# One mixture-of-experts kernel: the transposes of the next expert's rows, in blocks of eight or one by one between the gate/up matmuls

## The chip, the cores and the metric

The kernel runs on one core of one Trainium2 chip, in one launch. The metric is the time of the core in microseconds (us). The kernel before takes 2088.13 us, the median of 3 runs (2086.33 to 2092.45).

## The reference, cut to what matters

There are two stages. First an attention layer without values: the softmaxed scores of `ctx_512` (4 batches of 1024 rows) are multiplied by a tanh gate and added to `x` (4096 rows of 1024). Then each row goes through a mixture of experts:

```
logits = x @ gate_w.T                      # 64 experts
w, sel = top_k(softmax(logits), 8)
xin[e, slot] = x[tok]                      # up to 256 rows per expert
h   = silu(xin @ wg[e]) * (xin @ wu[e])    # 1024 -> 384
out = h @ wd[e]                            # 384 -> 1024
y[tok] += w * out
```

All inputs are float32. The result is `x + tanh(g) * y`. The change touches only the second stage.

## The kernel before, in words

**Attention and routing** (the first fifth of the time) compute the rows, the choice of experts and a table that says which row goes to which slot of which expert. The normalised rows are stored in DRAM as `h_rows`.

**The expert stage** goes through 64 experts one after the other. It keeps float32 accuracy with bf16 matmuls: every float32 operand is split into a high bf16 part and a low bf16 remainder, and three of the four products are summed (`PAIRS`, line 442). ScalarE (ACT) makes the high parts and VectorE (DVE) the low ones. For one expert `e`, in buffer set `u = e % 2`:

- GpSimd (POOL) gathers the 256 rows into `xg[u]` with two indirect DMAs (line 956), and at the end adds the expert's output rows into `out` (line 980).
- TensorE (PE) transposes those rows: 16 transposes of 128x128, in four quarters `q` of four (`turn`, line 431). Quarter `q` goes to the PSUM tile `ps_x[q % 2]`, so that two quarters fill both tiles and the third needs the first tile back. This happens while the expert before is being computed.
- ACT copies a turned quarter to bf16 (`turned_high`, line 621, instruction 623) and DVE makes its low part (`turned_low`, line 850, instruction 852). The latter increments `xT_out`, four times an expert; it is what frees the PSUM tile for PE.
- PE computes gate and up for three column groups `m` = 0, 1, 2 (`gate_up`, line 444): 48 matmuls of 256 columns each (8 `k` steps, 3 pairs, for gate and for up), and increments `gu_done` on the last one. Group `m` of expert `e` has its own PSUM tile `ps_gu[m]`.
- ACT computes silu of the group (`silu`, line 617, instruction 619) and DVE multiplies it with up, and splits the product (`activate`, line 841, instructions 846 to 848).
- PE computes the down projection (`down`, line 469, instruction 463): 36 matmuls of 512 columns. ACT scales the results (`rows_out`, line 625).

**The order on PE** of one expert (lines 487 to 493) is: group m = 0 (48 matmuls), transposes of quarters 0 and 1 of expert `e + 1` (8), group m = 1 (48), transposes of quarters 2 and 3 (8), group m = 2 (48), down (36). Before the transposes of a quarter PE waits twice (lines 433 and 435): until the rows are gathered, and until `xT_out` has reached `4 * e + q - 1`, where `e` is the expert whose rows are turned. For q = 2 this says that DVE is done with quarter 0 of the same expert, for q = 0 that it is done with quarter 2 of the expert before.

Each engine works through its own list in order; nothing overtakes. The lists of ACT and DVE aren't touched by the change. For one expert they are

```
# ACT, lines 638 to 654                    # DVE, lines 856 to 871
down_high(e, 0); down_high(e, 1)           down_low(e, 0); down_low(e, 1)
silu(e, 0)                                 activate(e, 0)
turned_high(e+1, q=0), (q=1)               turned_low(e+1, q=0), (q=1)
gate_high(e+1, 0), (1)                     gate_low(e+1, 0), (1)
silu(e, 1)                                 activate(e, 1)
turned_high(e+1, q=2), (q=3)               turned_low(e+1, q=2), (q=3)
up_high(e+1, 0)                            up_low(e+1, 0)
silu(e, 2)                                 activate(e, 2)
up_high(e+1, 1); rows_out(e)               up_low(e+1, 1)
```

Here `silu(e, m)` waits for `gu_done` of group m, `activate(e, m)` for that silu, `turned_high` for the transposes of its quarter, and `turned_low` for `turned_high`. The sync queue (SP) loads the weights of later experts (lines 340 to 348), behind the low parts that free their buffers.

Of the kernel before, what the change touches and what calls it, by code (L numbers as in the profile page):

```python
# [30 lines left out]
P = 128  # L31
# [44 lines left out]
def flamingo_moe(nc, x, ctxT, mask, kpm, g_x, g_f, wqT, bqT, wkT, bkT, gwT, wg, wu, wd, out):  # L76
    B, CP, CC, S = ctxT.shape
    T, H = x.shape
    E, _, KH, I = wg.shape
    MI = I // P  # L80
    TB = S // P
# [12 lines left out]
    with ExitStack() as ctx:  # L94
        def sem(name):
            return ctx.enter_context(nc.semaphore(name))

        def sb(name, shape, dt, where=ctx):
            return where.enter_context(nc.sbuf_tensor(name, shape, dt))
# [5 lines left out]
        ident = sb("ident", [P, P], F32)  # L105
# [58 lines left out]
        xg = [sb(f"xg{u}", [P, 2, HW], F32) for u in range(2)]  # L164
# [55 lines left out]
        gathered = [sem(f"gathered{u}") for u in range(2)]  # L220
        wcol_ready = sem("wcol_ready")
        xT_done = sem("xT_done")
        xT_high = sem("xT_high")
        xT_out = sem("xT_out")
# [21 lines left out]
        ps_x = [ps(f"ps_x{i}", [P, 2, CAP], F32, ctx) for i in range(2)]  # L246
# [7 lines left out]
        def attention_done(eng):  # L254

            eng.wait_ge(routed, N)
            for i in range(4):
                eng.wait_ge(x1_stored[i], 16 * N // 4)
                eng.wait_ge(h_stored[i], 16 * N // 4)
# [99 lines left out]
        def _(pe):  # L359
# [68 lines left out]
                    project(g // TB + 1, g % TB)  # L428


            def turn(e, u, q, first=False):

                pe.wait_ge(gathered[u], 16 * (e - u) + 32)
                if not (first and q < 2):
                    pe.wait_ge(xT_out, 4 * e + q - 1)
                for kk in range(2):
                    for half in range(2):
                        at = (2 * q + kk) * P
                        mm = pe.transpose(ps_x[q % 2][:, kk, half * P:(half + 1) * P], xg[u][:, half, at:at + P], ident[:])  # L439
                mm.then_inc(xT_done, 1)  # L440

            PAIRS = ((0, 0), (0, 1), (1, 0))

            def gate_up(e, u, m, first=False):
                if not first:
                    pe.wait_ge(act_ready, MI * e - MI + m + 1)
                for t, w in ((0, split_g[u]), (1, split_u[u])):
                    if m == 0:
                        pe.wait_ge((g_low, u_low)[t], 2 * e + 2)
                    for k in range(KH):  # L450
                        if m == 0 and t == 0 and k % 2 == 0:
                            pe.wait_ge(xT_out, 4 * e + k // 2 + 1)
                        for wi, xi in PAIRS:
                            mm = pe.matmul(ps_gu[m][:, t, :], w[:, wi, k, m * P:(m + 1) * P], xT[u][:, k, xi, :],  # L454
                                           start=(k == 0 and (wi, xi) == (0, 0)),
                                           stop=(k == KH - 1 and (wi, xi) == (1, 0)))
                mm.then_inc(gu_done, 1)

            def down_part(u, n, ms):
                half, c = n // 2, n % 2  # L460
                for m in ms:
                    for wi, ai in PAIRS:
                        mm = pe.matmul(ps_d[n % 3][:], act[u][:, ai, m, half * P:(half + 1) * P],  # L463
                                       split_d[:, wi, m, c * NH:(c + 1) * NH],
                                       start=(m == 0 and (wi, ai) == (0, 0)),
                                       stop=(m == MI - 1 and (wi, ai) == (1, 0)))
                return mm

            def down(e, u, first=False):

                pe.wait_ge(d_low, 2 * e + 2)
                pe.wait_ge(act_ready, MI * e + MI - 1)
                for n in range(2):
                    if not first:

                        pe.wait_ge(down_out, 4 * e - 2 * n)
                    down_part(u, n, range(MI - 1))
                pe.wait_ge(act_ready, MI * e + MI)
                for n in range(2):
                    down_part(u, n, [MI - 1]).then_inc(down_done, 1)  # L480
                if not first:
                    pe.wait_ge(down_out, 4 * e - 1)
                down_part(u, 2, range(MI)).then_inc(down_done, 1)
                pe.wait_ge(down_out, 4 * e + 1)
                down_part(u, 3, range(MI)).then_inc(down_done, 1)

            def expert(e, u, first=False, last=False):
                for m in range(MI):
                    gate_up(e, u, m, first)
                    if m < 2 and not last:  # L490
                        turn(e + 1, 1 - u, 2 * m)
                        turn(e + 1, 1 - u, 2 * m + 1)
                down(e, u, first)

            attention_done(pe)
            for q in range(4):
                turn(0, 0, q, True)
            expert(0, 0, True)
            with pe.Fori(0, E // 2 - 1) as i:
                expert(2 * i + 1, 1)  # L500
                expert(2 * i + 2, 0)
# [543 lines left out]
```

## Time and profile before

| | |
|---|---|
| median of 3 runs | 2088.13 us (2086.33 to 2092.45) |
| profiled execution | the page gives its span alone, 2089.3 us |
| PE busy | 1924.5 us, 92% |
| DVE busy | 1313.1 us, 63% |
| ACT busy | 1143.8 us, 55% |
| POOL busy | 811.9 us, 39% |
| PE transposes (line 439) | 1024, 273 ns each as recorded |
| PE gate/up matmuls (line 454) | 9216 of 256 columns, 273 ns each as recorded |
| PE down matmuls (line 463) | 2304 of 512 columns, 379 ns each as recorded |

The recorded duration of a matmul is its way through the array. Matmuls overlap, so what one costs is the distance between the starts of two neighbours. "PEld" is the loading of the stationary operand, which overlaps the matmul before. The time in brackets at the end of a timeline row is how long the engine stood idle before it, and on what.

### The profile page before, as it was taken

The numbers are of one execution on the slowest core, as the hardware profiler recorded it, in microseconds if no ns is written. First come the engines' busy times: TensorE is split into PE (matmuls) and PEld (weight loads), VectorE is DVE, ScalarE is ACT, GpSimd is POOL, SyncE is SP. The second block draws the span as 40 slices with busy tenths as digits, with TensorE's granted clock in tenths as the row PEclk, the third lists the DMA queues.
The fourth block names the chain that finished last, engine by engine and source line by source line (L and its number), as shares of the span: only waits on it lengthen the run. The fifth ranks groups of instructions, "written<-read, shape, count | busy, mean of one in ns | idle before, by whom it ended". The sixth has DMA issues, their size and how long they took to land.

```text
span 2089.3 us, 37900 instructions
## 1 busy us (share of the span) xinstructions
PE 1924.5 (92%) x13696; PEld 1429.0 (68%) x13760; DVE 1313.1 (63%) x2221; ACT 1143.8 (55%) x1507; POOL 811.9 (39%) x751
## 2 busy tenths in 40 slices
PE   7777777529999999999999999999999999999998
PEld 3444444427777777777777777777777777777775
DVE  5766666536666666666666666666666666666663
ACT  5555555425555555555555555555555555555553
POOL 0788788762323332333232333322222322332321
PEclk9999997659999999999999999999999999999999
DMA  5465443227888888888888888888888888888883
GB/s 219 150 237 185 134 137 134 94 77 248 272 275 276 279 277 279 276 278 276 264 264 267 270 266 270 275 276 278 278 278 278 278 278 266 264 266 269 267 269 74
DMA packets 90632, 501.27 MB, mean 240 GB/s; under 512 B 17761, under 2 KB 19553, under 8 KB 65505
## 3 DMA queue, kind: packets, MB, share of 16 engines
q1 hardware_dynamic: 45536, 362.24, 43.7%
q0 software_dynamic: 45056, 138.58, 29.9%
q8 instruction: 16, 0.26, 0.1%
q14 instruction: 24, 0.19, 0.0%
HBM read 396.69 MB, written 104.07 MB: 240 GB/s over the span
## 4 chain that ended last, share of the span: by engine, by line
PE 78%; POOL 11%; issue 8%; DMA 1%; POOLq 0%; DVE 0%; ACT 0%; SPq 0%; DVEq 0%
PE ps_gu L454 48%; PE ps_d L463 24%; POOL place_table L923 10%; PE ps_x L439 5%; POOL norm L916 1%; PE ps_j L369 0%; PE ps_s L380 0%; DMA b_qk<-in_bqT 0%; PE ps_t L369 0%; DMA xg<-h_rows,g_idx 0%; POOLq L923 0%; DMA place_table<-token_no,where 0%; POOLq L94 0%; DMA table<-place_table 0%; DVE xb L792 0%
## 5 line engine op out<-in xcount | busy, mean ns | idle before, releaser
L980 POOL DMA_INDIRECT out<-ob,s_idx x128 | 207.2, 1619 | 1051.5 <-ACT ob L632 1029.8
L454 PE MATMUL ps_gu<-xT,split_g 128*128 128x256 bf16 x4608 | 536.2, 273 | 0.0
L454 PE MATMUL ps_gu<-xT,split_u 128*128 128x256 bf16 x4608 | 534.4, 273 | 0.0
L463 PE MATMUL ps_d<-split_d,act 128*128 128x512 bf16 x2240 | 493.9, 379 | 3.4
L454 PEld LDWEIGHTS ps_gu<-xT,split_g 128*128 128x128 bf16 x4608 | 451.9, 98 | 65.1
L454 PEld LDWEIGHTS ps_gu<-xT,split_u 128*128 128x128 bf16 x4608 | 450.9, 98 | 52.2
L838 DVE TENSOR_TENSOR split_d<-raw_d,split_d 128x1536 bf16<-128x1536 f32 x128 | 219.3, 1755 | 398.6 <-ACT split_d L615 398.6
L463 PEld LDWEIGHTS ps_d<-split_d,act 128*128 128x128 bf16 x2304 | 225.4, 98 | 258.2
L923 POOL DMA_INDIRECT place_table<-token_no,where x256 | 294.0, 1148 | 77.6 <-issue 77.3
L619 ACT ACTIVATE sil<-ps_gu 128x256 f32<-128x256 f32 x192 | 73.7, 384 | 445.3 <-PE ps_gu L454 445.3
L632 ACT ACTIVATE ob<-ps_d,wcol 128x512 f32<-128x512 f32 x256 | 171.3, 687 | 259.0 <-PE ps_d L463 259.0
L833 DVE TENSOR_TENSOR split_u<-raw_u,split_u 128x1536 bf16<-128x1536 f32 x128 | 225.0, 1758 | 16.8 <-ACT split_u L608 10.3
L828 DVE TENSOR_TENSOR split_g<-raw_g,split_g 128x1536 bf16<-128x1536 f32 x128 | 219.5, 1756 | 4.7 <-ACT split_g L601 4.5
L956 POOL DMA_INDIRECT xg<-h_rows,g_idx x128 | 184.1, 1438 | 74.9 <-POOL g_idx L953 51.9
L608 ACT ACTIVATE split_u<-raw_u 128x1536 bf16<-128x1536 f32 x128 | 189.3, 1480 | 0.0
L601 ACT ACTIVATE split_g<-raw_g 128x1536 bf16<-128x1536 f32 x128 | 182.8, 1484 | 4.2 <-DMA h_rows<-hrow 4.2
L615 ACT ACTIVATE split_d<-raw_d 128x1536 bf16<-128x1536 f32 x128 | 182.1, 1473 | 0.0
L852 DVE TENSOR_TENSOR xT<-ps_x,xT 128x512 bf16<-128x512 f32 x256 | 164.2, 682 | 24.2 <-ACT xT L623 24.2
L846 DVE TENSOR_TENSOR prod<-sil,ps_gu 128x256 f32<-128x256 f32 x192 | 80.8, 421 | 151.4 <-ACT sil L619 150.5
L439 PE MATMUL ps_x<-ident,xg 128*128 128x128 f32 x1024 | 134.5, 275 | 34.6 <-DMA xg<-h_rows,g_idx 34.0
L623 ACT ACTIVATE xT<-ps_x 128x512 bf16<-128x512 f32 x256 | 139.3, 595 | 33.2 <-PE ps_x L439 26.6
L439 PEld LDWEIGHTS ps_x<-ident,xg 128*128 128x128 f32 x1024 | 117.1, 142 | 36.7 <-issue 35.1
(86 smaller groups left out, 1426.0 us busy)
## 6 DMA issues: line engine op xcount, KB each, us to landing
raw_g<-in_wg SPq DMA_DIRECT2D x64, 1536.0 KB, 11.6
raw_u<-in_wu SPq DMA_DIRECT2D x64, 1536.0 KB, 15.7
raw_d<-in_wd SPq DMA_DIRECT2D x64, 1536.0 KB
h_rows<-hrow SPq DMA_DIRECT2D x34, 544.0 KB, 3.6
xb<-in_x SPq DMA_DIRECT2D x32, 512.0 KB, 5.0
out<-xb SPq DMA_DIRECT2D x32, 512.0 KB, 2.7
ctx_sb<-in_ctxT SPq DMA_DIRECT2D x4, 1024.0 KB, 8.7
place_table<-token_no,where POOLq DMA_INDIRECT x256
```

Source lines behind the costliest of these rows:

```text
L439: mm = pe.transpose(ps_x[q % 2][:, kk, half * P:(half + 1) * P], xg[u][:, half, at:at + P], ident[:])
L454: mm = pe.matmul(ps_gu[m][:, t, :], w[:, wi, k, m * P:(m + 1) * P], xT[u][:, k, xi, :], start=(k == 0 and (wi, xi) == (0, 0)), stop=(k == ...
L463: mm = pe.matmul(ps_d[n % 3][:], act[u][:, ai, m, half * P:(half + 1) * P], split_d[:, wi, m, c * NH:(c + 1) * NH], start=(m == 0 and (wi, ...
L601: s.activation(split_g[u][:, 0, ks], raw_g[u][:, ks], ACT.Copy).then_inc(g_high, 1)
L608: s.activation(split_u[u][:, 0, ks], raw_u[u][:, ks], ACT.Copy).then_inc(u_high, 1)
L615: s.activation(split_d[:, 0, :, cs], raw_d[:, :, cs], ACT.Copy).then_inc(d_high, 1)
L828: v.tensor_tensor(split_g[u][:, 1, ks], raw_g[u][:, ks], split_g[u][:, 0, ks], ALU.subtract).then_inc(g_low, 1)
L833: v.tensor_tensor(split_u[u][:, 1, ks], raw_u[u][:, ks], split_u[u][:, 0, ks], ALU.subtract).then_inc(u_low, 1)
L838: v.tensor_tensor(split_d[:, 1, :, cs], raw_d[:, :, cs], split_d[:, 0, :, cs], ALU.subtract).then_inc(d_low, 1)
L923: p.indirect_dma_start(out=place_table, out_offset=bass.IndirectOffsetOnAxis(ap=where8[u][:, k:k + 1].bitcast(U32), axis=0), in_=token_no[ ...
L956: p.indirect_dma_start(out=xg[u][:, half, :], out_offset=None, in_=h_rows, in_offset=bass.IndirectOffsetOnAxis(ap=g_idx[u][:, half:half + ...
L980: p.indirect_dma_start(out=out, out_offset=bass.IndirectOffsetOnAxis(ap=s_idx[u][:, half:half + 1].bitcast(U32), axis=0), in_=ob[u][:, hal ...
```

## The change

The diff replaces `turn`, which issued the four transposes of a quarter together, by `turn_one`, which issues one transpose `at` (0 to 15; quarter `at // 4`). The two waits stand ahead of the first transpose of a quarter and the increment of `xT_done` on its last, as before. `gate_up` now takes a list of transposes and issues one of them after every fifth of its 48 matmuls until the list is used up. Transposes 0 to 7 (quarters 0 and 1) go into group m = 0, behind its matmuls 5, 10, ... 40, and transposes 8 to 15 (quarters 2 and 3) into group m = 1, likewise. The 16 transposes of expert 0, ahead of the first matmul, stay together.

```diff
-            def turn(e, u, q, first=False):
-
-                pe.wait_ge(gathered[u], 16 * (e - u) + 32)
-                if not (first and q < 2):
-                    pe.wait_ge(xT_out, 4 * e + q - 1)
-                for kk in range(2):
-                    for half in range(2):
-                        at = (2 * q + kk) * P
-                        mm = pe.transpose(ps_x[q % 2][:, kk, half * P:(half + 1) * P], xg[u][:, half, at:at + P], ident[:])
-                mm.then_inc(xT_done, 1)
+            def turn_one(e, u, at):
+
+                q, k, half = at // 4, at // 2, at % 2
+                if at % 4 == 0:
+                    pe.wait_ge(gathered[u], 16 * (e - u) + 32)
+                    if not (isinstance(e, int) and e == 0 and q < 2):
+                        pe.wait_ge(xT_out, 4 * e + q - 1)
+                mm = pe.transpose(ps_x[q % 2][:, k % 2, half * P:(half + 1) * P],
+                                  xg[u][:, half, k * P:(k + 1) * P], ident[:])
+                if at % 4 == 3:
+                    mm.then_inc(xT_done, 1)
...
-            def gate_up(e, u, m, first=False):
+            def gate_up(e, u, m, first=False, turns=()):
                 if not first:
                     pe.wait_ge(act_ready, MI * e - MI + m + 1)
+                turns, n = list(turns), 0
...
+                            n += 1
+                            if not turns or n % TURN_EVERY:
+                                continue
+                            turn_one(e + 1, 1 - u, turns.pop(0))
+                assert not turns
                 mm.then_inc(gu_done, 1)
...
+            TURN_EVERY = 5
+            TURNS = (range(0, 8), range(8, 16), ())
+
             def expert(e, u, first=False, last=False):
                 for m in range(MI):
-                    gate_up(e, u, m, first)
-                    if m < 2 and not last:
-                        turn(e + 1, 1 - u, 2 * m)
-                        turn(e + 1, 1 - u, 2 * m + 1)
+                    gate_up(e, u, m, first, () if last else TURNS[m])
                 down(e, u, first)
 
             attention_done(pe)
-            for q in range(4):
-                turn(0, 0, q, True)
+            for at in range(16):
+                turn_one(0, 0, at)
```

## Rows read from the trace of the kernel before

**Rows 1.** The page, part 4: the chain that ended last, by engine.
```profile
PE 78%; POOL 11%; issue 8%; DMA 1%; POOLq 0%; DVE 0%; ACT 0%; SPq 0%; DVEq 0%
```

**Rows 2.** Windows: length, busy time of PE, PEld, DVE, ACT, POOL; then PE clock.
```profile
100.00:200.00 100.00, 73.67 (x307) 44.24 (x306) 66.91 (x250) 57.36 (x104) 81.47 (x72) 0.91 0.63 218
...
490.00:1500.00 1010.00, 1007.90 (x7804) 774.62 (x7843) 648.20 (x760) 569.69 (x681) 311.62 (x281) 1.00 0.84 273
1500.00:2040.00 540.00, 538.90 (x4185) 415.18 (x4204) 346.70 (x407) 305.90 (x365) 161.40 (x151) 1.00 0.84 271
```

**Rows 3.** Timeline of PE over one expert: start, length, what, count.
```profile
1223.32 2.78 PE L454 MATMUL ps_gu<-xT,split_g 128*128 128x256 bf16 x24
1225.94 2.78 PE L454 MATMUL ps_gu<-xT,split_u 128*128 128x256 bf16 x24
1228.56 1.04 PE L439 MATMUL ps_x<-ident,xg 128*128 128x128 f32 x8
1229.43 2.78 PE L454 MATMUL ps_gu<-xT,split_g 128*128 128x256 bf16 x24
...
1234.67 1.04 PE L439 MATMUL ps_x<-ident,xg 128*128 128x128 f32 x8
...
1241.00 7.72 PE L463 MATMUL ps_d<-split_d,act 128*128 128x512 bf16 x35
1248.55 0.71 PE L454 MATMUL ps_gu<-xT,split_g 128*128 128x256 bf16 x5
```

**Rows 4.** Timeline of ACT over the same expert.
```profile
1228.76 0.38 ACT L619 ACTIVATE sil<-ps_gu 128x256 f32<-128x256 f32 x1 [1.81 <-PE ps_gu L454]
1229.19 1.09 ACT L623 ACTIVATE xT<-ps_x 128x512 bf16<-128x512 f32 x2
...
1234.87 0.38 ACT L619 ACTIVATE sil<-ps_gu 128x256 f32<-128x256 f32 x1 [1.85 <-PE ps_gu L454]
```

**Rows 5.** Timeline of DVE over the same expert.
```profile
1229.27 0.42 DVE L846 TENSOR_TENSOR prod<-sil,ps_gu 128x256 f32<-128x256 f32 x1 [0.24 <-ACT sil L619]
1229.73 0.37 DVE L847 CAST act<-prod 128x256 bf16<-128x256 f32 x1
1230.13 0.42 DVE L848 TENSOR_TENSOR act<-prod,act 128x256 bf16<-128x256 f32 x1
1230.47 1.28 DVE L852 TENSOR_TENSOR xT<-ps_x,xT 128x512 bf16<-128x512 f32 x2
1231.68 3.43 DVE L828 TENSOR_TENSOR split_g<-raw_g,split_g 128x1536 bf16<-128x1536 f32 x2
...
1236.41 1.28 DVE L852 TENSOR_TENSOR xT<-ps_x,xT 128x512 bf16<-128x512 f32 x2
```

**Rows 6.** Timelines of DVE, PE and PEld: the one wait of PE for `xT_out`.
```profile
461.86 0.69 DVE L852 TENSOR_TENSOR xT<-ps_x,xT 128x512 bf16<-128x512 f32 x1 [22.79 <-ACT xT L623]
...
462.69 1.94 PE L439 MATMUL ps_x<-ident,xg 128*128 128x128 f32 x8 [0.65 <-DVE xT L852]
...
462.66 1.57 PEld L439 LDWEIGHTS ps_x<-ident,xg 128*128 128x128 f32 x8 [1.02 <-issue]
```

**Rows 7.** The gather of an expert's rows: POOL's timeline, and the landing times.
```profile
1228.25 1.75 POOL L956 DMA_INDIRECT xg<-h_rows,g_idx  x1 [0.84 <-POOL g_idx L953]
1230.31 1.15 POOL L956 DMA_INDIRECT xg<-h_rows,g_idx  x1 [0.31 <-issue]
...
DMA to landing us min/median/max: 10.0/12.9/15.0
```

**Rows 8.** Timeline of PE in the attention stage, behind two of its gaps.
```profile
217.33 1.09 PE L390 MATMUL ps_t<-ident,hrow 128*128 128x128 f32 x8 [2.74 <-ACT hrow L549]
218.26 1.88 PE L369 MATMUL ps_j<-ctx_sb,w_qk 128*128 128x512 f32 x4
...
292.64 1.10 PE L390 MATMUL ps_t<-ident,hrow 128*128 128x128 f32 x8 [2.42 <-ACT hrow L549]
293.58 3.19 PE L369 MATMUL ps_j<-ctx_sb,w_qk 128*128 128x512 f32 x4
```

## The prediction

> **What bounds the kernel now.** I began with the chain of waits [rows 1]: PE carries 78% of what ended last, and most of the rest (POOL, issue) belongs to the routing stage, which the change leaves alone. Then I asked for busy time by stretch [rows 2]. In the expert stage PE is busy 1007.90 of 1010.00 us and 538.90 of 540.00, at full clock (1.00); no other engine there passes 65%, since DVE has 648.20 of 1010. Last I laid out one expert [rows 3]. The starts follow each other without a gap. From 1225.94 to 1228.56 there are 24 matmuls in 2.62 us, 0.1092 us each; from 1228.56 to 1229.43 eight transposes in 0.87 us, 0.109 each. Expert to expert, 1223.32 to 1248.55, is 25.23 us. The 144 gate/up matmuls and 16 transposes at 0.1092 make 17.47; what is left, 7.76 us for 36 down matmuls, is 0.216 each. The rows show 35 of these because one record is missing; counting 36, nothing is left for idling. So in this stage PE never waits, it does the same number of instructions after the change, and every wait that is new to PE is paid in full, 63 times (once for each expert that has a successor). Nothing that becomes faster on ACT or DVE can pay it back.
>
> **Part 1: single transposes instead of blocks.** A single transpose is followed by a bf16 matmul and preceded by one. Both neighbourhoods exist already, at the two ends of each block of eight. Were either change of type dear, the block would take longer than eight steps; it takes 0.87 us, eight steps at 0.1092 being 0.874, and the second block is the same. I take zero. Per expert there are 4 changes of type now and 32 afterwards. Rounding of the rows hides at most 0.01 us in two changes, so 28 more are worth -0.14 to +0.14 us an expert, -9 to +9 us over 63.
>
> The rows give 0.109 us for a transpose of 128 float32 columns, as much as for a matmul of 256 bf16 columns [rows 3]; no row shows a transpose that stands alone, and I carry the same price over. The Trainium skill, page "TensorE: Matmul & The Clock Gate", section "Back-to-back issue gap", puts a warm matmul at its columns over 2.4 GHz and 2.5 ns, 56 ns for 128 columns; by that rule transposes would cost half, and the sum would be 55 us lower if it came to hold once they stand alone. The trace does not agree for float32 transposes in blocks; the sum goes by the trace.
>
> **Part 2: the end of group m = 0 moves back.** Its eight transposes now lie before its last matmul instead of behind it, so `gu_done` comes 8 x 0.109 = 0.87 us later. The same holds for m = 1. Waiting for it is ACT's silu, and ACT was idle for 1.81 and 1.85 us just before [rows 4]; DVE waited 0.24 us for silu [rows 5]. These engines start 0.87 us later and have no one behind them that PE needs before the next groups: the low parts of the gate weights, 1231.68 to 1235.11, end at 1235.98 and are wanted by the next expert at 1248.6. The shift itself costs nothing. What it feeds is part 3.
>
> **Part 3: the wait for quarter 2 moves forward.** This is the step that decides. Transpose 8 needs the PSUM tile of quarter 0, that is `xT_out` from DVE's `turned_low` of quarter 0. That instruction stands on DVE behind `activate(e, 0)`, and ACT's part of it behind `silu(e, 0)`. Both wait for the last matmul of group m = 0. It makes no difference that the transposes of quarter 0 are done 32 instructions (3.5 us) earlier than that.
>
> - Before: silu starts at 1228.76 [rows 4]. The multiply, cast and subtraction of `activate` start at 1229.27, 1229.73 and 1230.13, and `turned_low` of quarter 0 at 1230.47 [rows 5]. One of these takes 0.69 us [rows 6], so it is done at 1231.16, 2.40 us after silu's start. PE wanted that tile at 1234.67 [rows 3]: 3.5 us to spare.
> - After: silu starts 0.87 us later, and the whole chain with it, as each member waits for the one before. `turned_low` is done at 1232.03.
> - How fast PE comes back is seen once, at the start of the stage, on the same semaphore [rows 6]: DVE ends at 461.86 + 0.69 = 462.55, PE's weight load starts at 462.66 and the transpose at 462.69, 0.14 us behind DVE. So the transpose starts at 1232.17.
> - Group m = 1 starts at 1229.43 as before (48 matmuls and 8 transposes precede it in either order). The ninth transpose follows its fifth matmul and would start at 1229.43 + 5 x 0.109 = 1229.98.
>
> The stall is 1232.17 - 1229.98 = 2.19 us. In the trace of before it does not exist, so I bound it. From below: in group m = 1 the way from silu (1234.87) to the end of the first `turned_low` (1236.41 + 0.69) is 2.23 us and not 2.40; this would make the stall 2.02. From above: if the first weight load after the stop is not hidden and a second chain instruction is delayed by as much, some 0.14 us each going by the 0.14 of rows 6, 2.47. I take 2.19, since rows 4 and 5 are the very instructions in the very place. Times 63 this is 138 us; with the bounds 127 and 156.
>
> All that stands behind the waiting transpose on PE is held: 43 matmuls of m = 1, seven transposes, m = 2 and down. Nobody who waits for them feeds PE in time to shorten anything later, so the whole expert gets longer.
>
> **Part 4: the other waits that move.** Quarter 3 needs quarter 1's tile, done 0.6 us after quarter 0's; its transpose comes 24 instructions (2.6 us) after the stall, so it is free. Quarter 0 of the next expert is now wanted at the fifth matmul of m = 0 and needs quarter 2 of the current one, done during the previous expert, 12 us earlier (1236.41 + 0.69 against 1249.1). The gathered rows are wanted 4.7 us earlier too, at 1248.55 + 0.55 = 1249.1. The two gathers start at 1228.25 and 1230.31 and land after at most 15.0 us [rows 7], at 1245.3; 3.8 us remain, and the stall adds two more. All of these cost zero; the cover of the gather is the thinnest. No DMA and nothing on SP's or POOL's queue is moved, and the weights have 2 us more an expert to arrive.
>
> **Sum.** 0 + 0 + 138 + 0 = +138 us. The profiled span of 2089.3 us lies 1.2 us above the median of the runs and inside their spread, so about 2227 for a profile and 2088 + 138 = **2226 us** for the median, 6.6% slower. About 0.3% is what a measurement of this kernel can tell from no change.
>
> **Rivals.**
> - *The clock falls at the stalls.* PE was never idle in this stage and will be for 2.2 us per 27. In the attention stage the granted clock is 0.91 [rows 2], and the idle times there are of this order. Behind a gap of 2.74 us four recorded matmuls take 1.88 us; behind one of 2.42 us the same four take 3.19 [rows 8], the lower level of 1.2 GHz. So a gap this short can be followed by a fall, and a longer one need not be. Against it: the longer of the two gaps had none, and what is idle here is 2.2 us in 27, with matmuls packed densely on both sides, where the attention stage idles a quarter of its time [rows 2]. A fall loses 3.19 - 1.88 = 1.3 us there and some more behind it, say 1.7. If one stall in three has it, 21 x 1.7 = 36 us, 2262; if all have, 107 us, 2333. The Trainium skill says (same page, section "Part 4: PE-mode transpose") that transposes do not count as activity for the clock. In rows 8 the fall comes where transposes follow the gap, which agrees; here only one instruction in six behind the stall is a transpose, so the rule makes the fall less likely, not more.
> - *No stall: the time stays.* The place is PE's wait ahead of transpose 8. It costs nothing if `turned_low` of quarter 0 is done by 1229.84 instead of 1232.03, and from there on each 0.1 us later costs 6 us. This would need ACT and DVE to take the quarter before silu and `activate` of the group, which could be, as the transposes are ready 3.5 us before. For it: both engines idle just then. Against: their lists are fixed, and stand the other way. It gives 2088, within 0.3%.
> - *Single transposes are cheaper than in a block.* If each cost half of its 0.109 us, PE would save 16 x 0.055 = 0.87 us an expert, 55 us, and the time would be 2171, still slower. Against: the step at the ends of a block is no shorter than inside.
>
> **Chances.** The forecast 0.86, the clock 0.08, no stall 0.03, cheaper transposes 0.03. The bounds of the stall and of the changes of type run from 2088 + 127 - 9 = 2206 to 2088 + 156 + 9 = 2253; I stretch the upper end to 2262 to take in one fall in three. Slower by over 0.3%: 0.96; within: 0.03; faster: 0.01, for what I haven't thought of.
>
> **What would show it.** Right: in the profile after, PE waits for DVE's line 852 63 times, about 2.2 us each, all ahead of the transposes; two experts are 27.4 us apart; the clock stays 1.00; gate/up matmuls around single transposes still start every 0.109 us; ACT's wait for silu of m = 0 grows. Wrong: no such wait; a wait of PE for the gather; a clock under 1.00 in the expert stage; or steps over 0.109 us next to a transpose.

## The result and the profile after

The changed kernel takes 2222.53 us (median of 4 runs, 2219.55 to 2222.79), the kernel before, with a fourth run beside the three known, 2089.53 us. The ratio is 1.0632, 95% interval 1.0619 to 1.0645: 133 us slower. The forecast was 2226 us, with a range of 2206 to 2262. Of the executions behind the experiments below two were slow and stand in no ratio, one of the kernel before (2142.01 us) and one of run 7 (6388.31 us); why was not looked for.

In the changed kernel and in the runs the line numbers have moved. In the changed kernel silu is 626 (619 before), `turned_high` 630 (623), `activate` 853 to 855 (846 to 848), `turned_low` 859 (852), gate/up 456 (454), the transposes 438 (439) and down 470 (463); a run's own edit can shift them by a few more.

The page of the changed kernel, parts 1 and 4 (busy times; the chain that ended last by engine and by line):

```profile
PE 1942.4 (87%) x13760; PEld 1425.9 (64%) x13760; DVE 1303.2 (59%) x2221; ACT 1129.9 (51%) x1507; POOL 776.0 (35%) x751
...
PE 73%; POOL 11%; issue 9%; DVE 5%; ACT 1%; DMA 1%; DVEq 0%; POOLq 0%; SPq 0%; ACTq 0%
PE ps_gu L456 44%; PE ps_d L470 22%; POOL place_table L930 10%; PE ps_x L438 6%; DVE xT L859 2%; DVE prod L853 1%; ACT sil L626 1%; DVE act L854 1%; POOL norm L923 1%; PE ps_j L369 0%; PE ps_s L380 0%; DMA b_qk<-in_bqT 0%; DVE act L855 0%; DMA xg<-h_rows,g_idx 0%; POOLq L930 0%
```

The chain used to be PE's alone in the expert stage [rows 1]. Now 5% of the span are DVE's and 1% ACT's, and the lines named are the members of one path: silu, then multiply, cast and subtraction, then the low part of the turned rows. Those 6% are about as much as the whole change. PE's busy sum is larger (1942.4 against 1924.5) without more work: at each stop the last matmul's way through the array is no longer covered by the next one (63 times 0.164 us, 10 us), each restart takes 0.06 us more than a step (4 us, read below), and 64 records that were missing before are there.

PE's waits in the expert stage (microseconds in total, times, longest), and the stage by windows (length, busy PE, PEld, DVE, ACT, POOL, PE clock, DMA share, GB/s):

```profile
PE ps_x L438 <- DVE xT L859: 115.7, 62, 2.1
```

```profile
490.00:1500.00 1010.00, 940.87 (x7249) 714.01 (x7248) 592.58 (x703) 518.00 (x629) 264.36 (x259) 1.00 0.77 252
1500.00:2040.00 540.00, 502.69 (x3875) 381.63 (x3874) 315.66 (x374) 277.05 (x338) 143.68 (x140) 1.00 0.77 251
```

PE waits for one thing only, once per expert: DVE's line 859. The row has 62 of the 63 stops, since its window begins behind the first, at 475 us. PE was busy for 1007.90 of 1010 us before [rows 2]. The clock stayed at 1.00.

One expert on PE (start, length, what, count, idle time before; a step is the distance between the starts of two neighbours):

```profile
1204.48 0.71 PE L456 MATMUL ps_gu<-xT,split_g 128*128 128x256 bf16 x5
1205.02 0.27 PE L438 MATMUL ps_x<-ident,xg 128*128 128x128 f32 x1
1205.13 0.71 PE L456 MATMUL ps_gu<-xT,split_g 128*128 128x256 bf16 x5
...
1209.72 1.04 PE L456 MATMUL ps_gu<-xT,split_u 128*128 128x256 bf16 x8
1210.59 0.71 PE L456 MATMUL ps_gu<-xT,split_g 128*128 128x256 bf16 x5
1213.16 0.33 PE L438 MATMUL ps_x<-ident,xg 128*128 128x128 f32 x1 [1.86 <-DVE xT L859]
1213.33 0.71 PE L456 MATMUL ps_gu<-xT,split_g 128*128 128x256 bf16 x5
1213.87 0.27 PE L438 MATMUL ps_x<-ident,xg 128*128 128x128 f32 x1
...
1224.02 5.34 PE L470 MATMUL ps_d<-split_d,act 128*128 128x512 bf16 x24
```

Three readings. First, from 1204.48 to 1205.13, five matmuls and a transpose take 0.65 us, six steps of 0.109: a single transpose costs what one in a block does [rows 3], and the changes of type cost nothing. Second, group m = 1 starts at 1210.59; its fifth matmul is followed by the transpose at 1213.16 where 1210.59 + 5 x 0.109 = 1211.13 would have been due, a wait of 2.03 us. (The 1.86 in brackets counts from where the last matmul has left the array, 0.164 us later than its step.) Third, the first step behind the stop, 1213.16 to 1213.33, is 0.17 and not 0.109, 0.06 more.

ACT and DVE at the same place:

```profile
1210.79 0.38 ACT L626 ACTIVATE sil<-ps_gu 128x256 f32<-128x256 f32 x1 [2.68 <-PE ps_gu L456]
1211.07 1.08 ACT L630 ACTIVATE xT<-ps_x 128x512 bf16<-128x512 f32 x2
...
1238.11 0.38 ACT L626 ACTIVATE sil<-ps_gu 128x256 f32<-128x256 f32 x1 [2.68 <-PE ps_gu L456]
```

```profile
1211.30 0.42 DVE L853 TENSOR_TENSOR prod<-sil,ps_gu 128x256 f32<-128x256 f32 x1 [1.10 <-ACT sil L626]
1211.75 0.29 DVE L854 CAST act<-prod 128x256 bf16<-128x256 f32 x1
1212.08 0.43 DVE L855 TENSOR_TENSOR act<-prod,act 128x256 bf16<-128x256 f32 x1
1212.42 1.28 DVE L859 TENSOR_TENSOR xT<-ps_x,xT 128x512 bf16<-128x512 f32 x2
```

The chain of rows 4 and 5 is there member for member. ACT's idle time before silu has grown from 1.81 to 2.68 us, by the 0.87 us that the group ends later. DVE ends quarter 0 at 1212.42 + 0.69 = 1213.11; PE is back 0.05 us later. Counted from silu to silu (1210.79 to 1238.11), an expert takes 27.32 us in place of 25.24 (before, the 29 experts whose first matmuls start at 491.45 and at 1223.32 have that mean). 2.03 of waiting and 0.06 at the restart are 2.09 us, and 63 times 2.09 is 132 us of the 133.

### The profile page after: what moved, and what is told of

The parts are those of the page before. It is cut to its first block, busy times and chain, and to the rows that moved or that the text cites. A ratio compares the mean times of both kernels' runs of the same rounds, so it can differ in the third digit from the quotient of the medians.

```text
span 2221.1 us, 37964 instructions
## 1 busy us (share of the span) xinstructions
PE 1942.4 (87%) x13760; PEld 1425.9 (64%) x13760; DVE 1303.2 (59%) x2221; ACT 1129.9 (51%) x1507; POOL 776.0 (35%) x751
## 4 chain that ended last, share of the span: by engine, by line
PE 73%; POOL 11%; issue 9%; DVE 5%; ACT 1%; DMA 1%; DVEq 0%; POOLq 0%; SPq 0%; ACTq 0%
PE ps_gu L456 44%; PE ps_d L470 22%; POOL place_table L930 10%; PE ps_x L438 6%; DVE xT L859 2%; DVE prod L853 1%; ACT sil L626 1%; DVE act L854 1%; POOL norm L923 1%; PE ps_j L369 0%; PE ps_s L380 0%; DMA b_qk<-in_bqT 0%; DVE act L855 0%; DMA xg<-h_rows,g_idx 0%; POOLq L930 0%
## 5 line engine op out<-in xcount | busy, mean ns | idle before, releaser
L456 PE MATMUL ps_gu<-xT,split_g 128*128 128x256 bf16 x4608 | 593.8, 273 | 0.0
L456 PE MATMUL ps_gu<-xT,split_u 128*128 128x256 bf16 x4608 | 589.4, 273 | 0.0
L470 PE MATMUL ps_d<-split_d,act 128*128 128x512 bf16 x2304 | 507.7, 379 | 0.0
L438 PE MATMUL ps_x<-ident,xg 128*128 128x128 f32 x1024 | 282.2, 278 | 150.7 <-DVE xT L859 118.2
L438 PEld LDWEIGHTS ps_x<-ident,xg 128*128 128x128 f32 x1024 | 144.8, 142 | 179.7 <-DVE xT L859 133.0
L963 POOL DMA_INDIRECT xg<-h_rows,g_idx x128 | 176.2, 1376 | 74.9 <-POOL g_idx L960 51.9
```

Source lines behind the costliest of these rows:

```text
L438: mm = pe.transpose(ps_x[q % 2][:, k % 2, half * P:(half + 1) * P], xg[u][:, half, k * P:(k + 1) * P], ident[:])
```

## The experiments

The theory: PE pays for PSUM tile `ps_x[0]`, which DVE returns late because its lists and ACT's put it behind silu and `activate` of the group that PE is just finishing. The first rival: the 28 additional changes between float32 transposes and bf16 matmuls per expert cost 75 ns each, which would give the same sum. The second: what costs is that `gu_done` comes 0.87 us later. The third concerns the clock. Where an edit leaves lists of ACT or DVE in another order, the work is the same.

**1. Take the turned quarters first, on ACT and DVE; PE's list untouched**

```diff
 # ACT                                    # DVE
-silu(e, 0)                              -activate(e, u, 0, first)
 turned_high(e+1, 1-u, 0)                 turned_low(e+1, 1-u, 0)
 turned_high(e+1, 1-u, 1)                 turned_low(e+1, 1-u, 1)
+silu(e, 0)                              +activate(e, u, 0, first)
```

> Edit: the changed kernel, and on ACT and on DVE the two turned quarters 0 and 1 are taken ahead of silu / activate of group m = 0; PE's list is untouched, so all single transposes and their neighbours stay. Theory (returned tile): PE pays for the late return of quarter 0's PSUM tile. Now DVE starts on it when the low parts of the down weights are done, 5.72 us after the expert's first matmul, and ends at 6.5; PE asks for it at 6.66. No wait, or one under 0.1 us: 2089 to 2096 us. Rival (changes of type): the 133 us are 28 more changes between float32 transposes and bf16 matmuls per expert, 75 ns each; PE's list is the same, so 2222.

Measured: 2091.79 us, ratio to before 1.0006 (0.9995 to 1.0016). Windows of the stage, then DVE, then PE at one expert:

```profile
490.00:1500.00 1010.00, 1010.00 (x7847) 774.87 (x7845) 641.52 (x760) 565.23 (x681) 383.20 (x281) 1.00 0.84 273
```

```profile
1200.96 1.28 DVE L860 TENSOR_TENSOR xT<-ps_x,xT 128x512 bf16<-128x512 f32 x2
1202.16 0.41 DVE L854 TENSOR_TENSOR prod<-sil,ps_gu 128x256 f32<-128x256 f32 x1
```

```profile
1201.44 0.71 PE L456 MATMUL ps_gu<-xT,split_g 128*128 128x256 bf16 x5
1201.98 0.27 PE L438 MATMUL ps_x<-ident,xg 128*128 128x128 f32 x1
```

DVE has quarter 0 done at 1201.65, 0.33 us before PE's transpose. PE is busy for 1010.00 of 1010.00 us with every single transpose in its place. The whole 133 us hung on the order of two other engines. The rival of the changes of type is out.

**2 and 3. The same swap on one of the two engines**

> Edit: the changed kernel, and only ACT takes the turned quarters 0 and 1 ahead of silu(e, 0). DVE still works through activate(e, 0) first, which starts 0.51 us behind silu's start as before. Theory: DVE's part of the chain (multiply, cast, subtraction, turned_low) is untouched, so the tile comes back at the same time: 2218 to 2223 us. Rival (changes of type): 2222. A rival in which it is ACT's place in the list that matters would give about 2089.

> Edit: the changed kernel, and only DVE takes turned_low of quarters 0 and 1 ahead of activate(e, 0); ACT still does silu(e, 0) first. Theory: the way from silu's start is now 0.28 to turned_high, 0.60 for it, 0.13 to DVE and 0.69 there, 1.70 us in place of 2.32, so 0.62 us less of a wait of 2.03: 2222.5 - 63 * 0.62 = 2183 us. Rival (changes of type): 2222.

Measured: ACT's swap alone 2225.60 us (ratio 1.0653, 1.0624 to 1.0682), no different from the changed kernel within the intervals and 3 us above the range that was expected; DVE's alone 2177.20 (1.0413, 1.0381 to 1.0444), 6 us below what was expected. PE's wait with ACT's swap:

```profile
PE ps_x L438 <- DVE xT L860: 108.3, 58, 2.1
```

With DVE's swap, DVE, ACT and PE:

```profile
1219.01 1.29 DVE L859 TENSOR_TENSOR xT<-ps_x,xT 128x512 bf16<-128x512 f32 x2 [1.50 <-ACT xT L630]
```

```profile
1218.11 0.38 ACT L626 ACTIVATE sil<-ps_gu 128x256 f32<-128x256 f32 x1 [2.68 <-PE ps_gu L456]
1218.39 1.08 ACT L630 ACTIVATE xT<-ps_x 128x512 bf16<-128x512 f32 x2
```

```profile
1217.90 0.71 PE L456 MATMUL ps_gu<-xT,split_g 128*128 128x256 bf16 x5
1219.76 0.33 PE L438 MATMUL ps_x<-ident,xg 128*128 128x128 f32 x1 [1.14 <-DVE xT L859]
```

Moving ACT alone frees nothing, because the tile is then stuck behind DVE's multiply. Moving DVE alone takes 0.72 us off the wait of 2.03, which is 1.31 now: silu's start to the end of quarter 0 is 1218.11 to 1219.70, 1.59 us. I had expected 1.70, with 0.13 us from ACT to DVE; here it is 0.02 (1218.39 + 0.60 to 1219.01). 63 x 0.11 = 7 us, which accounts for the miss.

**4 and 5. One of the two halves of the change undone**

```diff
 for m in range(MI):
-    gate_up(e, u, m, first, () if last else TURNS[m])
+    gate_up(e, u, m, first, () if last or m == M else TURNS[m])     # M = 0, or M = 1
+    if m == M and not last:
+        for at in TURNS[m]:
+            turn_one(e + 1, 1 - u, at)
```

> Edit: the transposes of quarters 0 and 1 stand again as a block of eight behind group m = 0; those of quarters 2 and 3 stay single in m = 1, from its fifth matmul on. Theory: gu_done of m = 0 comes 0.87 us earlier and PE asks for the tile at the same place, so the wait is 2.40 + 0.31 + 0.05 - (0.87 + 0.66) = 1.23 us, with 0.06 at the restart 1.29: 2089.5 + 81 = 2171 us. Rival (changes of type): half of the single transposes are left, 2089.5 + 67 = 2156. A rival in which only the late gu_done costs: m = 0 has none of it now, 2156 or less.

> Edit: the transposes of quarters 0 and 1 stay single in group m = 0; those of quarters 2 and 3 stand again as a block of eight behind m = 1. Theory: gu_done of m = 0 is late by 0.87 us as in the changed kernel, but PE asks for the returned tile 49 instructions (5.3 us) after the last matmul of m = 0 and it is there after 2.7: no wait, 2089 to 2091 us. Rival (changes of type): half of the single transposes are left, 2156. Rival (late gu_done): 2156 to 2222.

Measured: block behind m = 0, single in m = 1: 2171.09 us (1.0378, 1.0347 to 1.0410). Single in m = 0, block behind m = 1: 2090.50 us (0.9995, 0.9985 to 1.0004). PE with the block behind m = 0:

```profile
1216.66 0.71 PE L456 MATMUL ps_gu<-xT,split_g 128*128 128x256 bf16 x5
1218.43 0.33 PE L438 MATMUL ps_x<-ident,xg 128*128 128x128 f32 x1 [1.07 <-DVE xT L862]
```

and the stage with the block behind m = 1:

```profile
490.00:1500.00 1010.00, 1010.00 (x7844) 774.61 (x7843) 636.74 (x760) 565.01 (x680) 285.70 (x280) 1.00 0.84 273
```

The wait is 1.22 us (1218.43 - 1216.66 - 0.55), where 1.23 was expected. Single transposes in m = 0 are free although `gu_done` of m = 0 is late; the second rival is out. The 133 us are not two halves: moving PE's request forward (m = 1) costs 80 us by itself, moving the end of m = 0 back costs nothing by itself and some 53 us more on top, since both eat the same slack of 3.5 us.

**6, 7 and 8. The request at other places of m = 1**

```diff
-if not turns or n % TURN_EVERY:
+if not turns or (n % TURN_EVERY if m == 0 else n < N0 or (n - N0) % STEP):   # 15 and 4, or 25 and 3
     continue
```

> Edit: the changed kernel, and in group m = 1 the eight single transposes stand behind matmuls 15, 19, ... 43 in place of 5, 10, ... 40. Theory: the tile is back 2.68 us after the start of the last matmul of m = 0; PE asks for it after 16 steps, at 1.75. Wait 0.93 us and 0.06 at the restart: 2089.5 + 63 * 0.99 = 2152 us. Rival (changes of type): as many as in the changed kernel, 2222.

> Edit: the changed kernel, and in group m = 1 the eight single transposes stand behind matmuls 25, 28, ... 46. Theory: PE asks after 26 steps, at 2.84 us, and the tile is back at 2.68: no wait, 2089 to 2092 us. Rival (changes of type): as many as in the changed kernel, 2222. If single transposes cost or save anything at all beside a wait, this run shows it against before: 1 ns a change would be 2 us.

> Edit: both of the above together: ACT and DVE take quarters 0 and 1 ahead of silu / activate of m = 0, and the single transposes of m = 1 stand behind matmuls 25, 28, ... 46. Theory: two cures of one wait, nothing is left for the second: 2089 to 2092 us. It tells whether the new order on ACT and DVE has a price of its own: activate(e, 0) is some 0.3 us later, which nobody waits for.

Measured: from matmul 15, 2153.72 us (1.0298, 1.0280 to 1.0317); from 25, 2090.91 (0.9993, 0.9983 to 1.0003); from 25 with the new order on ACT and DVE, 2091.32 (0.9997, 0.9987 to 1.0007). PE, from 15:

```profile
1204.76 1.80 PE L456 MATMUL ps_gu<-xT,split_g 128*128 128x256 bf16 x15
1207.34 0.33 PE L438 MATMUL ps_x<-ident,xg 128*128 128x128 f32 x1 [0.78 <-DVE xT L859]
```

and the stage from 25:

```profile
490.00:1500.00 1010.00, 1010.00 (x7843) 774.53 (x7842) 641.65 (x760) 560.85 (x681) 286.39 (x281) 1.00 0.84 273
```

The wait falls by one step of 0.109 us for each matmul that the request moves back: 2.03 at five, 0.94 at 15 (1207.34 - 1204.76 - 1.64), none at 25. With all 16 transposes single and no wait, the time is that of before within 0.2%; single transposes neither cost nor save. Beside that cure, the new order on ACT and DVE makes no difference.

**9 and 10. The tile returned later still**

```diff
 # ACT, behind silu(e, 0)
+gate_high(e+1, 1-u, 0, ...)          # run 9; run 10 moves part 1 up as well
 turned_high(e+1, 1-u, 0)
 turned_high(e+1, 1-u, 1)
-gate_high(e+1, 1-u, 0, ...)
 gate_high(e+1, 1-u, 1, ...)
```

> Edit: the changed kernel, and ACT does one of the two gate_high copies (1.43 us) ahead of the turned quarters 0 and 1, so that the tile comes back later still. Theory: from silu's start 0.28 + 1.43 to turned_high, 0.60 for it, 0.02 to DVE and 0.69 there, 3.02 us in place of 2.32, so the wait grows from 2.03 to 2.73 us, and with 0.06 at the restart 2089.5 + 63 * 2.79 = 2265 us, clock 1.00. Rival (the clock falls at stalls, no longer at 2.0 us but at longer ones): each fall adds some 1.7 us, 2372 if all stalls have one, and the granted clock of the stage is under 1.00.

> Edit: as the run before, with both gate_high copies ahead of the turned quarters. Theory: the wait is 2.73 + 1.43 = 4.16 us, 2089.5 + 63 * 4.22 = 2355 us if the clock stays. Rival (the clock falls at longer stalls): a 4.2 us stop is longer than the gaps of 2.42 us and more that the attention stage shows ahead of a fall; if every stall has one, 107 us more, 2462. I expect here, unlike in the run before, some falls.

Measured: 2301.89 us (1.1001, 1.0983 to 1.1020) and 2437.61 us (1.1655, 1.1636 to 1.1675), both above what the wait alone gives. Run 9 by windows (the last three numbers are PE clock, DMA share, GB/s): a stretch behind one stall, and the whole expert that follows, whose stall has no fall; then PE around the first of them:

```profile
1190.10:1193.50 3.40, 3.40 (x19) 2.60 (x17) 2.58 (x2) 0.00 (x0) 0.00 (x0) 0.50 1.01 425
...
1209.10:1237.07 27.97, 25.41 (x197) 19.32 (x196) 16.12 (x19) 14.04 (x17) 7.08 (x7) 1.00 0.76 246
```

```profile
1185.58 0.71 PE L456 MATMUL ps_gu<-xT,split_g 128*128 128x256 bf16 x5
1188.80 0.33 PE L438 MATMUL ps_x<-ident,xg 128*128 128x128 f32 x1 [2.51 <-DVE xT L859]
...
1190.47 1.27 PE L456 MATMUL ps_gu<-xT,split_g 128*128 128x256 bf16 x5
1191.53 0.42 PE L438 MATMUL ps_x<-ident,xg 128*128 128x128 f32 x1
...
1193.91 0.71 PE L456 MATMUL ps_gu<-xT,split_u 128*128 128x256 bf16 x5
1194.45 0.27 PE L438 MATMUL ps_x<-ident,xg 128*128 128x128 f32 x1
```

The wait is 2.68 us (expected 2.73). Behind it, five matmuls take 1.06 us (1190.47 to 1191.53) and not 0.54: the clock is at its lower level of 1.2 GHz. By the granted clock behind each stall, 24 of the 63 are followed by a fall. An expert with one takes 29.63 us, one without 27.97, so a fall costs 1.66 us. 63 x (27.97 - 25.24) + 24 x 1.66 = 212 us; measured are 210 above the kernel before beside it (2091.58). In run 10, PE at one stall, its clock at the end of the stop, and the stage:

```profile
996.30 0.71 PE L456 MATMUL ps_gu<-xT,split_g 128*128 128x256 bf16 x5
1000.89 0.48 PE L438 MATMUL ps_x<-ident,xg 128*128 128x128 f32 x1 [3.88 <-DVE xT L859]
1001.16 1.27 PE L456 MATMUL ps_gu<-xT,split_g 128*128 128x256 bf16 x5
1002.23 0.42 PE L438 MATMUL ps_x<-ident,xg 128*128 128x128 f32 x1
```

```profile
1000.50:1001.00 0.50, 0.11 (x1) 0.11 (x2) 0.50 (x2) 0.10 (x1) 0.00 (x0) 0.50 1.19 506
490.00:1500.00 1010.00, 880.18 (x6393) 660.71 (x6423) 528.26 (x621) 459.49 (x559) 234.34 (x231) 0.94 0.69 224
```

The wait is 4.05 us (expected 4.16), and all 63 stalls have a fall. In the first four PE comes back at the full level and the clock falls behind the restart, as in run 9, and an expert takes up to 31.01 us; in the others the clock is at the lower level when the waiting transpose starts (0.50 from 1000.50 to 1001.00). An expert then takes 30.72 us: 25.24, 4.05 of waiting, and 1.43 for the fall and the restart. That is less than the 1.66 of run 9, as part of the time at the lower level now lies in the stop, where PE has nothing to slow down. The theory's mechanism holds for the wait in both runs, and its time is too low, because in both it left out the clock; for run 9 I had not expected falls.

## Why the prediction was right

- *What bounds the kernel.* Right. PE had no slack in the stage, so the 2.09 us per expert went through in full, 132 of 133 us.
- *Part 1, single transposes at zero.* Right, and now shown apart from the wait: with all of them single, runs 1, 7 and 8 give ratios of 1.0006, 0.9993 and 0.9997. The neighbourhoods at the ends of a block were a sound measure. The step of a single float32 transpose is 0.109 us. The 56 ns that the Trainium skill gives for 128 columns (page "TensorE: Matmul & The Clock Gate", section "Back-to-back issue gap") do not hold for it, alone or in a block. (With 56 ns a transpose the time would have been lower by 16 x 63 x 0.053 = 53 us, an estimate from that page; the 55 in the prediction goes by half of the measured step.)
- *Part 2, the later end of the groups, zero by itself.* Right (run 5). ACT's idle time before silu took up the 0.87 us.
- *Part 3, the wait for quarter 2.* The mechanism was right in place, releaser and number of times. The size was 2.19 us, measured 2.03 and 0.06 more at the restart, 2.09. Two terms were a little too large. From silu to the end of quarter 0 it takes 2.32 us and not 2.40, mostly because DVE's cast takes 0.29 and not 0.37; why it is shorter was not settled. And PE is back 0.05 us behind DVE, not 0.14; the row I took that from was recorded at the lower clock. A third term, the first step behind the stop, I had only in the upper bound. Together -0.10 us, 63 times -6 us. That the forecast was only 3.5 us too high is in part luck: the median of before came out 1.4 us higher with the fourth run, and 1.3 of the 133 us lie outside the 63 stalls, where I looked for nothing.
- *Part 4, gather, quarter 3 and quarter 0 of the next expert at zero.* Right: PE waits for nothing but line 859.
- *The rivals.* No stall: it would have needed the other order on ACT and DVE, and with that order it is what happens (run 1). Cheaper transposes: no (run 7). The clock: it did not fall in the changed kernel in 63 stalls of 2.03 us, but the rival was nearer than its chance of 0.08 says. 0.65 us more of waiting, and 24 of the 63 stalls have a fall (run 9), at 1.66 us each where I had put 1.7. My reasons against it, the dense matmuls on both sides above all, would have been wrong there. What I read from rows 8 about transposes behind a gap says nothing either way: both gaps are followed by eight transposes, and only one of them by a fall.

## What to carry to other kernels

When an instruction is moved, look up every tile that it needs back, and through which instructions of which engines' lists it comes; spreading work evenly over an engine's list moves the first request for such a tile forward even where the work itself is free. Take the slack from the trace before moving: here 3.5 us lay between the return of the tile and its request, and the change used up 4.7 of request and 0.9 of return. The same wait has three equal cures, which the runs priced alike: ask later, release earlier on both engines, or leave that half alone; none is faster than before, since PE is full without them.

## What the runs showed of the hardware that was not expected

The step from stops without a fall to stops that always have one is narrow. Stops of 0.94, 1.22, 1.31 and 2.03 us in this dense stage had none of 63 followed by a fall; 2.68 us had 24 of 63, in a regular order of every second or third; 4.05 us had all 63. The stops within one run are the same length, so the length alone does not decide at 2.68 us; what else does was not tried. PE also restarts fast at full clock: the transpose starts 0.05 us after the releasing DVE instruction ends (1213.11 to 1213.16), and the first step behind it adds 0.06 us to the wait.
